# Ranking edges in layer 0 of a graph network: a row range for each partition, counted on VectorE

## The chip, the core and the metric

The kernel runs on one core of one Trainium2 chip. The metric is the device time of one launch in microseconds (us).

## The reference, cut to what matters

There are 12,500 nodes with 128 features and 412,500 edges (200,000 drawn ones in both directions, and a loop at every node), sorted by their destination `dst`. The sources `src` are in no order.

```python
x = layernorm(x + L0(x, edge_index, edge_weight))      # layer 0
x = layernorm(x + L1(x, edge_index, edge_weight, edge_attr_50))   # layer 1

# layer 0: gather by src, sum by dst
agg = segment_sum(edge_weight[:, None] * x[src], dst, N)
L0  = relu((x + agg) @ W1 + b1) @ W2 + b2

# layer 1: gather by dst, sum by src
W   = softplus_less_log2(softplus_less_log2(attr @ nn_w1.T + nn_b1) @ nn_w2.T + nn_b2) * c[:, None]
msg = W * h1[dst]                      # h1 = x @ lin1_w.T
agg = segment_sum(msg, src, N)
L1  = (h1 + agg) @ lin2_w.T + lin2_b
```

Layer 1 sums by the unsorted index `src`. So its messages are written to DRAM sorted into 98 buckets of 128 nodes (`src >> 7`), and summed from there. Which DRAM row each edge's message goes to is its rank, and the ranks are worked out while layer 0 runs.

## The kernel before

The edges are cut into 403 tiles of 1,024 edges, each tile being 8 columns (`SUB`) of 128 partitions. The edges of layer 0 are the block at L354 to L607 in `edge_network_kernel`; every engine has its own loop over the tiles, and semaphores tie them together. A tile falls nearly always into one window of 42 destination nodes. For one tile t of layer 0:

- GpSimd (POOL, L424 to L438) issues eight indirect DMAs at L434, each a gather of 128 rows of x into `xg[s]`. Gather s of tile t waits until the matmul that used `xg[s]` in tile t-1 is done (semaphore `summed`, L433), and the first gather of each half until ScalarE has written the indices `gidx` (L413).
- TensorE (PE) goes in this order: two groups of eight counting matmuls (L465 and L467, 128x100 bf16), the eight matmuls that sum the weighted rows into the window (L477; `summed` goes up by one for each), the two halves of the edge network's first layer (L483, 128x512 f32, on `attr`, which SyncE loads at L373), and three matmuls whose result nobody reads (`spin`, L631).
- ScalarE writes `gidx` (L413) and computes a softplus by Abs, Exp and Ln (L397 to L401) on the result of L483.
- VectorE (DVE, L549 to L595) makes `oha`, the one-hot of each edge's bucket (L555, 8 x 100 bf16), the one-hot of the destinations (L566, eight times), adds the window to `aggT` (L502), does the ranking (L577 to L590), writes `hid` (L509, twice), and in the first three of the four parts counts one bucket of the next part (L708).
- SyncE (SP) stores `hid` (L365), clears blocks of the table (L378) and loads `attr` (L373). They stand in program order on its queue.

The ranking before: `seen[p, b]` is the next free row of bucket b, the same in every partition. The matmuls at L465 with the strictly triangular `lower` give `above`, how many edges of bucket b lie in this tile on a lower partition. The ones at L467 with `ones16` give `in_tile`, how many there are in the tile. VectorE waits for both (semaphore `counted`, L579) and then:

```python
ahead = above + seen                    # L581, PSUM <- PSUM, SBUF
count[NB:] = pair * fixed_earlier       # L583
seen = seen + in_tile                   # L585, SBUF <- SBUF, PSUM
count[:NB] = oha * tall(ahead)          # L587, 128x800
rank = sum(count)                       # L590, 128x864 -> 128x8
```

At the start of each of the four parts of about 101 tiles, `plan_part` (PE L442 to L451, DVE L511 to L538) lays out the buckets' blocks in the table, and sets `seen` to the first row of each bucket. `counts[p, b]` holds, for each partition on its own, how many edges of bucket b its columns of that part have (L708, `count_bucket`).

Layer 1 (`layer1_edges`, L988 to the end of the function) has one tile loop too. PE computes the second layer of the edge network (L1128) and picks h1 by a one-hot (L1139); ScalarE makes a softplus (L1185 to L1189); VectorE makes the messages; POOL scatters them by rank with eight indirect DMAs a tile (L1232). From tile 105 on, the sorted rows are also summed: VectorE L1314 (one-hots, two SBUF inputs) and L1325, PE L1158.

## Time and profile before

| what | us |
|---|---|
| median of 3 runs | 11676.23 |
| lowest and highest run | 11665.03, 11705.83 |
| profiled execution, span from first to last instruction | 11664.8 |
| layer 0, edges | about 155 to 5200 |
| nodes between the layers | about 5200 to 5400 |
| layer 1, edges, without and with sums | about 5400 to 6820, 6820 to 11110 |
| layer 1, remaining sums, then nodes | about 11110 to 11665 |

The profile gives no time of the profiled execution other than its span; the span is 11.4 us below the median of the runs and equals the lowest of them within 0.3 us. Busy time is given by engine: PE is the matmul side of TensorE, PEld its weight loads, SPq are DMA issues of SyncE. In a timeline, `[3.47 <-PE bank L467]` says that the engine sat idle for 3.47 us before this instruction and what, by the profile's inference, ended that. "remote" is a releaser that the profile could not name.

### The profile page before, as it was taken

What the parts mean: (1) busy time and instruction counts of PE and PEld (TensorE: products, weight loads), DVE (VectorE), ACT (ScalarE), POOL (GpSimd) and SP (SyncE); (2) the same over time, 40 slices, a digit from 0 to 9 for tenths busy, and PEclk for the clock granted to TensorE, in tenths of its full rate; (3) what the DMA queues carried; (4) which work ended last, traced back from release to release, by engine and by line L of the source; (5) the groups of instructions that cost most, each with busy time, mean ns of one, the idle gap of its engine ahead of it and who ended that gap; (6) DMA issues with size and microseconds to landing.
All of it is one profiled execution on the core that took longest, in us unless ns stands there. A gap on an engine that the chain in (4) does not pass through costs nothing. (4 is left out here: it accounts for less than half of the span.)

```text
span 11664.8 us, 216512 instructions
## 1 busy us (share of the span) xinstructions
PE 6895.8 (59%) x38816; PEld 4956.1 (42%) x38817; DVE 6516.8 (56%) x20428; ACT 3390.7 (29%) x6781; POOL 6346.0 (54%) x6541
## 2 busy tenths in 40 slices
PE   2555566565555666665444456666666666666666
PEld 1333333333333333334232345555555555555566
DVE  7666666666666655555333345555555555555555
ACT  2333333333333333334222222222222222222202
POOL 3666566665666566652555555555555565555500
PEclk8777776777777777778776678888888888888887
DMA  3333343433333333443333344444444444444444
GB/s 101 124 121 123 119 124 122 124 121 120 122 124 121 120 124 123 124 122 123 99 100 98 100 133 150 149 149 156 150 152 146 151 156 148 157 151 151 153 155 151
DMA packets 803242, 1533.31 MB, mean 131 GB/s; under 512 B 193070, under 2 KB 206820, under 8 KB 802707
## 3 DMA queue, kind: packets, MB, share of 16 engines
q1 hardware_dynamic: 593415, 1093.58, 28.8%
q0 software_dynamic: 209456, 436.16, 13.0%
q10 hardware_dynamic: 348, 3.33, 0.1%
q14 instruction: 17, 0.14, 0.0%
q8 instruction: 6, 0.10, 0.0%
HBM read 967.92 MB, written 564.58 MB: 131 GB/s over the span
## 5 line engine op out<-in xcount | busy, mean ns | idle before, releaser
L1232 POOL DMA_INDIRECT sorted_messages<-rows,sidx x3224 | 3261.3, 1012 | 2621.7 <-DVE sidx L1279 1433.0
L434 POOL DMA_INDIRECT xg<-x_rows,gidx x3224 | 3043.0, 944 | 2134.8 <-PE bank L477 1112.7
L483 PE MATMUL bank<-attr,nn 128*128 128x512 f32 x1612 | 1494.2, 1082 | 1764.1 <-DMA attr<-attr_cols 1501.9
L1158 PE MATMUL bank<-hot,block_rows 128*128 128x128 f32 x9312 | 1586.3, 341 | 248.6 <-DVE hot L1314 140.7
L1185 ACT ACTIVATE soft<-bank 128x512 f32<-128x512 f32 x806 | 481.4, 597 | 4079.1 <-remote 2654.4
L1158 PEld LDWEIGHTS bank<-hot,block_rows 128*128 128x128 f32 x9312 | 1507.6, 254 | 299.4 <-issue 285.2
L1128 PE MATMUL bank<-w_nn2T,e_hid 128*128 128x128 f32 x6448 | 1057.4, 309 | 610.4 <-DMA e_hid<-hidden 349.0
L483 PEld LDWEIGHTS bank<-attr,nn 128*128 128x128 f32 x1612 | 468.9, 321 | 2225.7 <-issue 2061.2
L1285 DVE SCALAR_TENSOR_TENSOR rows<-filt,meta,bank 128x128 f32<-128x128 f32 x3224 | 916.6, 344 | 809.7 <-remote 534.8
L1128 PEld LDWEIGHTS bank<-w_nn2T,e_hid 128*128 128x128 f32 x6448 | 977.4, 219 | 816.7 <-DMA e_hid<-hidden 481.1
L397 ACT ACTIVATE soft<-bank 128x512 f32<-128x512 f32 x808 | 475.4, 588 | 2751.7 <-issue 1841.9
L1139 PE MATMUL bank<-h1w,ohT 128*128 128x128 bf16 x3224 | 345.3, 272 | 1429.6 <-DVE ohT L1261 959.1
L631 PE MATMUL bank<-bias_b,ones 128*128 128x512 bf16 x3627 | 1167.0, 455 | 34.8 <-issue 33.9
L477 PE MATMUL bank<-onehot,xg 128*128 128x42 f32 x6448 | 860.7, 287 | 236.1 <-DMA xg<-x_rows,gidx 199.6
L1276 DVE SCALAR_TENSOR_TENSOR filt<-bank,soft 128x512 f32<-128x512 f32 x806 | 555.6, 689 | 695.4 <-issue 349.6
L581 DVE TENSOR_TENSOR bank<-bank,seen 128x100 f32<-128x100 f32 x403 | 109.1, 271 | 1456.1 <-remote 869.2
L477 PEld LDWEIGHTS bank<-onehot,xg 128*128 128x128 f32 x6448 | 793.6, 195 | 272.5 <-DMA xg<-x_rows,gidx 227.4
L1139 PEld LDWEIGHTS bank<-h1w,ohT 128*128 128x128 bf16 x3224 | 267.6, 122 | 1498.8 <-issue 1353.5
L1314 DVE TENSOR_TENSOR hot<-cols,block_rows 128x512 f32<-128x512 f32 x1167 | 801.7, 687 | 153.1 <-DMA block_rows<-sorted_messages 111.2
L631 PEld LDWEIGHTS bank<-bias_b,ones 128*128 128x128 bf16 x3627 | 423.5, 118 | 856.3 <-issue 691.0
L566 DVE TENSOR_SCALAR onehot<-cols,rel,wgt 128x42 f32<-128x42 f32 x3224 | 729.2, 333 | 0.0
L1325 DVE TENSOR_TENSOR aggT<-aggT,bank 128x128 f32 x1164 | 330.4, 284 | 699.7 <-issue 458.6
(182 smaller groups left out, 8173.3 us busy)
## 6 DMA issues: line engine op xcount, KB each, us to landing
block_rows<-sorted_messages SPq DMA_DIRECT2D x389, 792.0 KB
hidden<-hid SPq DMA_DIRECT2D x404, 512.0 KB
e_hid<-hidden SPq DMA_DIRECT2D x403, 512.0 KB
sorted_messages<-zero SPq DMA_DIRECT2D x403, 264.0 KB
dstb<-dst SPq DMA_DIRECT2D x403, 256.0 KB
attr<-attr_cols SPq DMA_DIRECT2D x403, 204.0 KB
xg<-x_rows,gidx POOLq DMA_INDIRECT x3224
sorted_messages<-rows,sidx POOLq DMA_INDIRECT x3224
```

Of the source, the lines that this page charges most:

```text
L434: pool.indirect_dma_start(xg[s][:, :], None, x_rows, bass.IndirectOffsetOnAxis(ap=gidx[s // HALF][:, s % HALF:s % HALF + 1], axis=0),).the ...
L477: nc.tensor.matmul(bank[0][:, 0:WIN], xg[s][:, :], onehot[:, s, :], start=(s == 0), stop=(s == SUB - 1)).then_inc(summed, 1)
L483: nc.tensor.matmul(bank[2 + h][:, :], nn1[:, :], attr[:, h, :], start=True, stop=True).then_inc(z1_set, 1)
L566: ins = dve.tensor_scalar(onehot[:, s, :], cols[:, 0:WIN], rel[:, s:s + 1], wgt[:, ds(here + s, 1)], ALU.is_equal, ALU.mult)
L631: nc.tensor.matmul(unread[:, :], ones3[:, :], bias3["b2"][:, :], start=True, stop=True)
L1128: ins = nc.tensor.matmul(bank[2 + h][:, s * P:s * P + P], hid[:, h, s * P:s * P + P], nn2T[:, :], start=False, stop=(s == HALF - 1))
L1139: ins = nc.tensor.matmul(bank[4 + h][:, s * P:s * P + P], ohT[:, at:at + P], h1w[:, :], start=True, stop=True)
L1158: ins = nc.tensor.matmul(sums[u][:, 0:P], block_rows[k][:, u, s, 0:D], hot[u][:, s, :], start=(s == 0), stop=(s == HALF - 1))
L1232: pool.indirect_dma_start(table, bass.IndirectOffsetOnAxis(ap=sidx[b][h][:, s:s + 1], axis=0), rows[b][h][:, s, :], None).then_inc(landed[ ...
L1276: dve.scalar_tensor_tensor(filt[h][:, :], bank[2 + h][:, :], 0.0, soft2[h][:, :], ALU.max, ALU.add).then_inc(filt_set, 1)
L1285: ins = dve.scalar_tensor_tensor(rows[b][h][:, s, 0:D], filt[h][:, part], meta[:, ds(here + (h * HALF + s), 1), 1], bank[4 + h][:, part], ...
L1314: dve.tensor_tensor(hot[u][:, :, :], cols[:, :].rearrange("p (o n) -> p o n", o=1).broadcast_to([P, HALF, P]), block_rows[k][:, u, :, D:D ...
```

## The change

In each bucket every partition gets a row range of its own. `plan_part` gets one more matmul, f32, `lower` times `counts`: for each partition the number of edges of bucket b that lower partitions have in the whole part. `seen` starts at the bucket's first row plus that number. From then on a partition needs only its own edges: `in_tile[p, b]` is the sum of `oha` over the tile's 8 columns, a reduction on VectorE with the view turned round, and the count is `oha * seen`, with both inputs in SBUF. The sixteen matmuls at L465 and L467, the semaphore `counted` and its two waits, and the add at L581 are gone. `seen` is raised after the rank is reduced.

```diff
-PLAN_STEPS = 9
+PLAN_STEPS = 10
-        lower = sb("lower", [P, P], bf16)
+        lower = sb("lower", [P, P], f32)
...
+                in_tile, block_start = sb2("in_tile", [P, NB], f32), sb2("block_start", [P, NB], f32)
...
-                above, in_tile = bank[6][:, 0:NB], bank[6][:, P:P + NB]
-                fixed_cols, ahead = bank[7][:, 0:NB], bank[7][:, P:P + NB]
+                fixed_cols = bank[7][:, 0:NB]
...
                             pe.wait_ge(plan, PLAN_STEPS * q + 3)
+                            nc.tensor.matmul(bank[5][:, 400:400 + NB], lower[:, :], counts[:, 0:NB], start=True, stop=True)
...
-                        nc.tensor.matmul(bank[0][:, 0:WIN], lower[:, :], zero16[:, 0:WIN], start=True, stop=True).then_inc(summed, SUB)
+                        nc.tensor.matmul(bank[0][:, 0:WIN], ones16[:, :], zero16[:, 0:WIN], start=True, stop=True).then_inc(summed, SUB)
...
                                 windows = jobs.windows()
-                                pe.wait_ge(oha_set, t + 1)
-                                pe.wait_ge(seen_set, t + 1)
-                                for s in range(SUB):
-                                    nc.tensor.matmul(above, lower[:, :], oha[:, s, :], start=(s == 0), stop=(s == SUB - 1))
-                                for s in range(SUB):
-                                    ins = nc.tensor.matmul(in_tile, ones16[:, :], oha[:, s, :], start=(s == 0), stop=(s == SUB - 1))
-                                ins.then_inc(counted, 1)
                                 with pe.Fori(0, windows):
...
                             dve.wait_ge(seen_set, q * PT + 1)
-                            dve.wait_ge(ahead_set, q * PT)
-                            dve.tensor_scalar(seen[:, :], bank[5][:, 128:128 + NB], float(BLOCK), float(base_row), ALU.mult, ALU.add).then_inc(plan, 1)
+                            dve.tensor_scalar(block_start[:, :], bank[5][:, 128:128 + NB], float(BLOCK), float(base_row), ALU.mult, ALU.add).then_inc(plan, 1)
...
                             dve.wait_ge(plan, PLAN_STEPS * q + 7)
+                            dve.tensor_tensor(seen[:, :], block_start[:, :], bank[5][:, 400:400 + NB], ALU.add).then_inc(plan, 1)
...
                                 dve.wait_ge(rank_set, t + 1)
-                                dve.wait_ge(counted, t + 1)
                                 dve.tensor_tensor(oha[:, :, :], tall(fixed_cols, NB), wide(bucket16[:, ds(here, SUB)], NB),
                                                   ALU.is_equal).then_inc(oha_set, 1)
...
-                                dve.wait_ge(counted, t + 2)
                                 dve.wait_ge(seen_set, t + 1)
-                                dve.tensor_tensor(ahead, above, seen[:, :], ALU.add).then_inc(ahead_set, 1)
+                                dve.wait_ge(oha_set, t + 1)
+                                dve.tensor_tensor(count[:, :, 0:NB], oha[:, :, :], tall(seen[:, :], NB), ALU.mult).then_inc(count_set, 1)
                                 dve.wait_ge(pair_set, 2 * t + 1)
                                 dve.tensor_tensor(count[:, :, NB:PAIRS], pair[:, :, :], fixed_earlier, ALU.mult).then_inc(pair_set, 1)
-                                dve.wait_ge(ahead_set, t + 1)
-                                dve.tensor_tensor(seen[:, :], seen[:, :], in_tile, ALU.add).then_inc(seen_set, 1)
-                                dve.wait_ge(oha_set, t + 1)
-                                dve.tensor_tensor(count[:, :, 0:NB], oha[:, :, :], tall(ahead, NB), ALU.mult).then_inc(count_set, 1)
+                                dve.tensor_reduce(in_tile[:, :], oha[:, :, :].rearrange("p s n -> p n s"), axis=AX.X, op=ALU.add).then_inc(tile_set, 1)
                                 dve.wait_ge(pair_set, 2 * t + 2)
                                 dve.wait_ge(count_set, t + 1)
                                 dve.tensor_reduce(rank[:, ds(here, SUB)], count[:, :, :], axis=AX.X, op=ALU.add).then_inc(rank_set, 1)
+                                dve.wait_ge(tile_set, t + 1)
+                                dve.tensor_tensor(seen[:, :], seen[:, :], in_tile[:, :], ALU.add).then_inc(seen_set, 1)
```

## Rows read from the trace of the kernel before

**Rows 1.** The page of the profile: the span.

```profile
span 11664.8 us, 216512 instructions
```

**Rows 2.** By stretch: us, PE, PEld, DVE, ACT, POOL, each busy (x), clock, DMA, GB/s.

```profile
160.00:3912.00 3752.00, 2232.45 (x11700) 1333.32 (x11700) 2404.85 (x6614) 1200.05 (x2392) 2261.66 (x2397) 0.72 0.40 123
3912.00:5200.00 1288.00, 795.31 (x4040) 473.44 (x4039) 725.23 (x2081) 413.33 (x824) 778.18 (x824) 0.71 0.39 122
5400.00:6820.00 1420.00, 637.77 (x3329) 439.39 (x3328) 534.02 (x2179) 404.79 (x828) 798.74 (x832) 0.71 0.32 99
6820.00:11110.00 4290.00, 2720.33 (x16711) 2262.92 (x16711) 2303.32 (x8062) 1167.66 (x2388) 2461.64 (x2393) 0.81 0.48 151
```

**Rows 3.** Timeline, layer 0, two tiles: start, busy us, engine, line.

```profile
2009.85 0.52 PE L467 MATMUL bank<-oha,ones 128*128 128x100 bf16 x8
...
2011.82 0.27 DVE L581 TENSOR_TENSOR bank<-bank,seen 128x100 f32<-128x100 f32 x1 [3.47 <-PE bank L467]
...
2012.30 0.98 DVE L587 TENSOR_TENSOR count<-oha,bank 128x800 f32<-128x800 bf16 x1
2012.63 0.94 POOL L434 DMA_INDIRECT xg<-x_rows,gidx  x1 [2.73 <-PE bank L477]
...
2017.64 1.78 DVE L566 TENSOR_SCALAR onehot<-cols,rel,wgt 128x42 f32<-128x42 f32 x8
...
2020.53 0.22 DVE L577 TENSOR_TENSOR pair<-bucket 128x64 f32 x1 [0.72 <-issue]
...
2021.36 0.94 POOL L434 DMA_INDIRECT xg<-x_rows,gidx  x1 [0.30 <-issue]
...
2025.04 0.94 POOL L434 DMA_INDIRECT xg<-x_rows,gidx  x1 [2.73 <-PE bank L477]
```

**Rows 4.** Timeline, layer 0, a tile whose last gather landed late.

```profile
4426.19 0.94 POOL L434 DMA_INDIRECT xg<-x_rows,gidx  x1 [0.30 <-issue]
...
4426.79 0.52 PE L467 MATMUL bank<-oha,ones 128*128 128x100 bf16 x8
...
4429.01 0.27 DVE L581 TENSOR_TENSOR bank<-bank,seen 128x100 f32<-128x100 f32 x1 [4.03 <-remote]
...
4429.82 0.94 POOL L434 DMA_INDIRECT xg<-x_rows,gidx  x1 [2.69 <-PE bank L477]
...
4431.77 0.42 PE L477 MATMUL bank<-onehot,xg 128*128 128x42 f32 x2 [2.90 <-DMA xg<-x_rows,gidx]
```

**Rows 5.** Groups by line, layer 0, 300 to 3900 us (288 tiles).

```profile
L434 POOL DMA_INDIRECT xg<-x_rows,gidx x2303 | 2173.1, 944 | 1425.9 <-PE bank L477 789.2 <-issue 629.1 <-remote 7.3
...
L590 DVE TENSOR_REDUCE rank<-count 128x864 f32 x288 | 303.2, 1053 | 55.0 <-DVE count L587 55.0
...
L587 DVE TENSOR_TENSOR count<-oha,bank 128x800 f32<-128x800 bf16 x287 | 281.3, 980 | 0.0
...
L465 PE MATMUL bank<-oha,lower 128*128 128x100 bf16 x2304 | 178.4, 229 | 5.8 <-DVE oha L555 5.8
...
L467 PE MATMUL bank<-oha,ones 128*128 128x100 bf16 x2304 | 160.5, 215 | 0.0
...
L581 DVE TENSOR_TENSOR bank<-bank,seen 128x100 f32<-128x100 f32 x287 | 77.7, 271 | 999.7 <-remote 529.7 <-PE bank L467 469.6 <-issue 0.3
L585 DVE TENSOR_TENSOR seen<-seen,bank 128x100 f32<-128x100 f32 x287 | 73.5, 256 | 0.0
```

**Rows 6.** Group of L1314, layer 1, 6820 to 11110 us.

```profile
L1314 DVE TENSOR_TENSOR hot<-cols,block_rows 128x512 f32<-128x512 f32 x897 | 616.1, 687 | 40.9 <-issue 29.5 <-remote 11.2
```

**Rows 7.** Timeline, layer 1: a VectorE instruction with two SBUF inputs and a POOL issue.

```profile
8027.23 0.69 DVE L1314 TENSOR_TENSOR hot<-cols,block_rows 128x512 f32<-128x512 f32 x1
8027.30 1.45 POOL L1232 DMA_INDIRECT sorted_messages<-rows,sidx  x1 [0.30 <-issue]
```

**Rows 8.** Timeline, layer 0: the same meeting, with a short instruction.

```profile
4076.86 0.23 DVE L577 TENSOR_TENSOR pair<-bucket 128x64 f32 x1 [1.29 <-issue]
4076.91 0.99 POOL L434 DMA_INDIRECT xg<-x_rows,gidx  x1 [0.30 <-issue]
```

More of the change, by code:

```diff
@@ L332, in edge_network_kernel @@
                 flushed, rel_set, passed, passed_sp = sem("flushed"), sem("rel_set"), sem("passed_pool"), sem("passed_sp")
-                oha_set, counted, ahead_set, seen_set, pair_set, count_set, rank_set = (
-                    sem(n) for n in ("oha_set", "counted", "ahead_set", "seen_set", "pair_set", "count_set", "rank_set"))
-                above, in_tile = bank[6][:, 0:NB], bank[6][:, P:P + NB]
-                fixed_cols, ahead = bank[7][:, 0:NB], bank[7][:, P:P + NB]
+                oha_set, tile_set, seen_set, pair_set, count_set, rank_set = (
+                    sem(n) for n in ("oha_set", "tile_set", "seen_set", "pair_set", "count_set", "rank_set"))
+                fixed_cols = bank[7][:, 0:NB]
                 fixed_earlier = bank[7][:, 2 * P:2 * P + SUB * SUB].rearrange("p (s r) -> p s r", s=SUB)
@@ L451, in plan_part @@
                             nc.tensor.matmul(bank[4][:, 0:SLOTS], ones16[0:NB, :], at_or_past[0:NB, :], start=True, stop=True).then_inc(planned, 1)
-                        nc.tensor.matmul(bank[0][:, 0:WIN], lower[:, :], zero16[:, 0:WIN], start=True, stop=True).then_inc(summed, SUB)
+                        nc.tensor.matmul(bank[0][:, 0:WIN], ones16[:, :], zero16[:, 0:WIN], start=True, stop=True).then_inc(summed, SUB)
                         for h in range(2):
                             nc.tensor.matmul(bank[2 + h][:, :], ident[:, :], zero[:, 0:HE], start=True, stop=True).then_inc(z1_set, 1)
-                        pe.sem_inc(counted, 1)
                         jobs = TileTable(pe, "pe0", nwin)
@@ L535, in plan_part @@
                             dve.scalar_tensor_tensor(used[:, :], bank[4][:, 0:SLOTS], NB - 0.5, slot_rows[:, :], ALU.is_lt, ALU.mult).then_inc(plan, 1)
-                            dve.wait_ge(plan, PLAN_STEPS * q + 8)
+                            dve.wait_ge(plan, PLAN_STEPS * q + 9)
                             dve.tensor_single_scalar(slot_row[:, at], used[:, :], float(base_row), ALU.add).then_inc(plan, 1)
```

## The prediction

> **What bounds the kernel now.** I first cut the span of 11664.8 us [rows 1] by stretch. The change touches only layer 0, where 300 tiles (2397 gathers and their neighbours on POOL, eight a tile) take 3752 us, 12.5 us a tile, in the first three parts, and 103 tiles take 1288 us, 12.5 us again, in the last one [rows 2]. No engine is busy all the time: per tile of the first stretch PE is busy 2232.45/300 = 7.4 us, VectorE 2404.85/300 = 8.0 us, ScalarE 4.0 us, POOL 7.5 us [rows 2]. In the last part VectorE has a whole microsecond less to do (725.23/103 = 7.0 us, since L708 is gone) and the tile takes as long as before. So VectorE is not the bound, and a microsecond of slack on it is worth nothing.
>
> Then I read the timeline for what repeats. POOL's gathers stand 1.25 us apart (0.944 us busy [rows 5] and 0.30 us of issue), seven steps from 2012.63 to 2021.36 = 8.73 us, and the next tile's first gather starts 3.68 us after the last one, at 2025.04 [rows 3]. That makes 12.41 us: POOL's ring alone is the tile. POOL's idle 2.73 us is put down to PE's L477, and VectorE's 3.47 us at L581 to the counting matmuls L467. The second looks as if counting were the delay. But the counting matmuls had ended at 2009.85 + 0.52 = 2010.37, 1.45 us before L581 started [rows 3]. In another place they ended at 4427.31 and L581 started 1.70 us later [rows 4]. What stays fixed is the distance from the last gather's start: 4426.19 to L581 at 4429.01 is 2.82 us, to the next first gather 3.63 us. And that first gather (4429.82) went out before PE had even got the last gathered tile: L477 waited for it until 4431.77 [rows 4]. So the release of both comes late and together, about 2.8 us behind the last gather's start, whatever PE is doing; what holds it I can't name from the trace.
>
> **The change part by part.**
> - *Sixteen matmuls less on PE.* (178.4 + 160.5)/288 = 1.18 us a tile [rows 5]. They lie in the time in which the release is being held. Worth 0 if the release stays tied to the last gather, at most 1.18 us a tile if it is tied to PE's queue. I take 0, because rows 3 and 4 show the same 12.4 us with PE at different places.
> - *VectorE's wait for `counted` goes.* Its idle at L581 is 999.7/287 = 3.48 us a tile [rows 5]. Behind it stand the rest of the ranking, the two `hid` writes and L708, and SyncE's store of `hid` waits for those. All of it moves ahead. What is late next on VectorE is L566, which waits for the eighth `summed` of the tile before, released in the same burst. So VectorE's idle moves to L566 and PE's and SyncE's slack grows. Value: 0.
> - *VectorE's own work.* L581 goes (0.27 us). L587 keeps its 800 elements (0.98 us). L585 stays (0.26 us) with both inputs in SBUF. New is the reduction of 128x800 bf16 to 128x100 with a stride of 100 elements. No row shows it: the nearest is L590, 864 elements in 1.053 us [rows 5], which makes 0.98 us for 800; below, half of that if bf16 goes at double rate; above, twice, 2.0 us, if the stride halves the rate. I take 0.98. VectorE then has 8.03 - 0.27 + 0.98 = 8.74 us in a tile of 12.4, and at the upper bound 9.8 us. Even with some 1 us of gaps that fits, and the work is off the ring. If the cover of 3.48 us were gone, it would cost 0.71 us a tile.
> - *The layout at the start of a part.* One more f32 matmul and one more add, four times in the run. Eight bf16 matmuls of 100 columns take 0.52 us [rows 3], so one f32 one is below that, with the add (0.27 us) under 1 us: at most 4 us in all, 0 to 0.03%. I take 2 us.
> - *The operands of L587.* This is what I expect to be felt. `ahead` was in PSUM and `seen` is in SBUF, so L587 now reads two SBUF operands, and so does the add to `seen`. Before, L587 ran from 2012.30 to 2013.28 across the start of a gather at 2012.63, which took its usual 0.94 us [rows 3]. In layer 1 the instruction L1314 has both inputs in SBUF. One that ran from 8027.23 to 8027.92 had a POOL issue start within it, and that issue took 1.45 us [rows 7] where the mean without such company is 798.74/832 = 0.960 us [rows 2]: 0.49 us longer, for 0.62 us that L1314 still had to run. Layer 0 has the small version: L577, both inputs in SBUF, ran until 4077.09, and the gather that began at 4076.91 took 0.99 us and not 0.94 [rows 8]; 0.18 us left, 0.05 us paid. So an issue that starts inside such an instruction is stretched by what is left of it less about 0.13 us. Gathers are issued back to back, so each stretch lengthens the ring.
>
> How much a tile? Below: 0, if L587 fits between two starts, which stand 1.25 us apart. Above: 0.98 - 0.13 = 0.85 us. The mean comes from layer 1: with sums beside it, L1232 has 2461.64/2393 = 1.029 us against 0.960 [rows 2], so 8 x 0.069 = 0.55 us a tile, for 897/299 = 3 instructions of 0.687 us [rows 6], 2.06 us. That is 0.27 us paid for each us of such work. Here the new work is 0.98 + 0.26 = 1.24 us a tile, so 0.33 us, x 403 = 134 us. Phase: VectorE restarts at L566 when the eighth `summed` arrives, L577 comes 2.89 us after L566 (2017.64 to 2020.53 [rows 3]) and L587 a few tenths later. With the release 0.8 us before the first gather and an unknown 0.5 to 1 us from release to L566, L587 starts 2.8 to 4.0 us after the first gather. The starts in reach are at 3.74 us and 4.99 us: of that stretch about two thirds meets one. That is why I take the mean and neither end.
>
> The Trainium skill's page "SBUF — State Buffer", section "Who interferes with whom", says that a VectorE instruction with two SBUF inputs contends with a GpSimd instruction that reads SBUF, but infers that tensor_tensor does not hold up descriptor generation, which would need the write interface. The 1.45 us of a POOL issue beside L1314 speaks against that inference; by it this term would be 0 and the time that of the kernel before.
>
> Sum against the profiled execution: 11664.8 + 134 + 2 = 11801 us. The median of the runs shown is 11 us above that span, so 11812 us; I say 11810.
>
> **The rivals.**
> - *Nothing to be measured (within 0.3%, 35 us).* The ring is as before and L587 falls between two starts, or the stretch does not apply to it. For: the free place is 0.4 us of every 1.25, and the phase may lock into it. Against: rows 7 and 8. Time 11664.8 + 11 + 2 = 11678 us. By the page's inference it would be this too.
> - *Faster.* The release is tied to how far PE's queue has come, and the trace hides that. For: PE's L467 is named as releaser in half of the waits at L581 [rows 5], and L477 at POOL's. Against: 12.4 us in both places of rows 3 and 4. It decides where PE, with 1.18 us less ahead of L477, lets go earlier: up to 1.18 us a tile, 403 x 1.18 = 475 us, with the 134 us given back -341. So 11200 us to 11340 us; in part of that, anything from there to 11640 us.
> - *VectorE becomes the bound.* It would need 12.4 - 8.74 - 1 = 2.7 us more than I count, beyond the upper bound of the reduction. Or the new order puts `hid` late for PE; it comes earlier here. Slower without a clear price, 1 in 20: at twice the reduction and the worst stretch, 403 x 0.85 = 343 us, 12020 us.
> - *The change doesn't do what it says*, since the rows of a bucket are spread by partition and layer 1's scatters and sums read them in another order. The bytes and the descriptors are the same, and the table is scattered by single rows either way. I give it no price.
>
> **How the numbers follow.** 0.3% is about what a measurement of this kernel can tell from no change. Slower by the stretch: 0.41, and by VectorE 0.03, together 0.44; no difference 0.26; faster 0.30. The likeliest is the stretch at its mean, 11810 us; its own range is 11715 to 12020. The range over the cases goes from 11290, inside the faster rival, to 11960, inside the upper end of the stretch, and leaves out about 1 in 10 on either side.
>
> **What would show it.** If I am right: PE's group L465 and L467 and VectorE's L581 are gone; L566 has the long idle time instead; the mean of L434 goes from 944 ns to about 985 ns, with one gather of each tile at 1.2 to 1.7 us and L587 in progress when it starts; the last gather to the next first one stays 3.6 to 3.7 us; L1232 keeps 0.96 and 1.03 us. The stretch is wrong if the mean of L434 stays at 944 ns while the tile stays at 12.4 us. The whole picture is wrong if the distance from the last gather to the next first one drops below 3.4 us: then PE's queue held the release. The reduction is mis-sized if it takes less than 0.5 or more than 2 us.

## The result, and the profile after

The changed kernel takes 11993.99 us (11975.99 to 12027.4, four runs), the kernel before in the same comparison 11691.03 us: a ratio of 1.0255, with an interval of 1.0234 to 1.0276. It is slower by 303 us. The forecast was slower, 11810 us and at most 11960 us; the sign was right, the growth more than twice what was said (303 us for 134 us). The experiments ran on several chips, on which the kernel before had medians of 11691 to 11814 us. So only ratios to the kernel before on the same chip are compared below.

The page of the changed kernel, its span and the busy time of the engines [rows 1 has the span before, 11664.8]:

```profile
span 11975.8 us, 202418 instructions
...
PE 6920.6 (58%) x32376; PEld 4931.7 (41%) x32377; DVE 6962.6 (58%) x20432; ACT 3393.7 (28%) x6781; POOL 6430.7 (54%) x6541
```

The stretches of layer 0, columns as in [rows 2]:

```profile
160.00:3912.00 3752.00, 2135.53 (x6510) 1247.89 (x6510) 2578.88 (x6239) 1131.38 (x2252) 2184.65 (x2257) 0.64 0.36 116
3912.00:5300.00 1388.00, 807.40 (x2488) 477.64 (x2487) 897.34 (x2212) 433.67 (x862) 839.06 (x863) 0.65 0.37 119
```

In 3752 us POOL now starts 2257 instructions and not 2397, eight a tile: 282 tiles and not 300, 13.3 us a tile and not 12.5. In the last part, where VectorE has no bucket to count (L699, which was L708), it is only 12.7 us. From its first gather to its last, layer 0 takes 5310 us and not 5041: 270 us of the 311 us by which the span grew. Another 34 us lie in layer 1's scatters, from 5710 to 5743 us, and these are not clear of variation: over the runs below that stretch takes 5712 to 5802 us, whatever the edit in layer 0. A scatter costs what it did, a mean of 1.02 to 1.03 us beside the sums ([rows 2]: 1.029 us):

```profile
L1223 POOL DMA_INDIRECT sorted_messages<-rows,sidx x2371 | 2438.0, 1028 | 1835.6 <-DVE sidx L1270 986.9 <-issue 708.1 <-ACT rows L1185 132.1
```

The groups by line of layer 0, 300 to 3900 us (before: [rows 5]; L434 is the gathers, L476 the edge network, which was L483, L573 the count, which was L587, L576 the new reduction, L558 the one-hot):

```profile
L434 POOL DMA_INDIRECT xg<-x_rows,gidx x2167 | 2097.9, 968 | 1503.1 <-issue 603.0 <-ACT gidx L413 328.5 <-PE bank L470 299.1
L476 PE MATMUL bank<-attr,nn 128*128 128x512 f32 x1083 | 997.4, 1076 | 691.2 <-DMA attr<-attr_cols 486.8 <-issue 158.8 <-DVE hid L502 45.5
...
L558 DVE TENSOR_SCALAR onehot<-cols,rel,wgt 128x42 f32<-128x42 f32 x2168 | 496.0, 324 | 551.4 <-remote 466.9 <-issue 49.5 <-PE bank L470 34.9
L576 DVE TENSOR_REDUCE in_tile<-oha 128x100 f32<-128x800 bf16 x271 | 407.1, 1502 | 0.0
...
L573 DVE TENSOR_TENSOR count<-oha,seen 128x800 f32<-128x800 bf16 x271 | 267.1, 986 | 1.7 <-issue 1.7
```

To be read here: the gathers have a mean of 968 ns and not 944 (0.19 us a tile), and 2167 of them fit in 3600 us, against 2303. Their idle time is no longer all at one place. Before, PE's L477 ended 789 us of it and no ScalarE line stood there; now L413 (`gidx`) ends 328 us. The reduction takes 1.50 us, a half more than the 0.98 us I took.

The stretch is there, as foretold, though not in every tile: a gather starts within L573 in 185 of the 403 tiles. L573 (two SBUF inputs) and such a gather:

```profile
2005.39 0.98 DVE L573 TENSOR_TENSOR count<-oha,seen 128x800 f32<-128x800 bf16 x1
...
2005.57 1.63 POOL L434 DMA_INDIRECT xg<-x_rows,gidx  x1 [0.31 <-issue]
```

What is new is in this timeline. The first gathers of three tiles are those at 2098.61, 2119.24 and 2129.87, so one tile took 20.6 us and the next 10.6 us:

```profile
2098.47 0.71 SPq L378 DMA_DIRECT2D sorted_messages<-zero  x1
...
2098.61 0.94 POOL L434 DMA_INDIRECT xg<-x_rows,gidx  x1 [0.30 <-issue]
...
2102.36 0.94 POOL L434 DMA_INDIRECT xg<-x_rows,gidx  x1 [0.30 <-issue]
2105.54 0.29 SPq L373 DMA_DIRECT2D attr<-attr_cols  x1
2105.59 0.23 DVE L545 TENSOR_SCALAR rel<-dstf,basef 128x8 f32 x1 [2.84 <-issue]
...
2106.33 0.94 POOL L434 DMA_INDIRECT xg<-x_rows,gidx  x1 [3.03 <-remote]
...
2111.86 3.78 PE L476 MATMUL bank<-attr,nn 128*128 128x512 f32 x4 [11.24 <-issue]
...
2113.96 0.60 ACT L397 ACTIVATE soft<-bank 128x512 f32<-128x512 f32 x1 [13.64 <-PE bank L476]
...
2118.15 0.46 ACT L413 ACTIVATE gidx<-srci 128x4 int32 x2 [0.46 <-issue]
...
2119.24 0.94 POOL L434 DMA_INDIRECT xg<-x_rows,gidx  x1 [8.22 <-ACT gidx L413]
...
2128.62 0.94 POOL L434 DMA_INDIRECT xg<-x_rows,gidx  x1 [0.30 <-issue]
...
2129.87 0.94 POOL L434 DMA_INDIRECT xg<-x_rows,gidx  x1 [0.30 <-issue]
```

SyncE's `attr` load (L373) goes out 7.07 us after its block clear (L378). PE gets to L476 only at 2111.86, after 11.24 us of idle time, ScalarE's softplus waits for that 13.64 us, `gidx` stands behind the softplus in ScalarE's order, and the next tile's first gather goes out at 2119.24 after 8.22 us. Before, this gap was 2.7 us in the tiles shown [rows 3, 4]. This long tile is no exception. I call the standard deviation of the tile lengths between 300 and 3900 us their spread: it was 0.6 us before and is 3.0 us now. Nine tiles in ten lay between 12.4 and 12.7 us and now lie between 10.0 and 19.1 us. Nor is it only the gap ahead of the first gather. On average the distance from a tile's last gather to the next first one even falls, from 3.7 to 3.4 us, while the seven steps between a tile's own gathers grow from 8.8 to 9.9 us, of which the stretch is 0.2 us. A gap of over 1 us stands between a tile's own gathers in 40% of the tiles, before in 4%. So the even tile of 12.4 us has given way to short and long tiles with a mean of 13.3 us.

### The profile page after: what moved, and what is told of

Same layout as the page of the kernel before. It is cut to its first block and busy times, and to the rows that moved or that the text cites. A ratio compares the mean times of both kernels' runs of the same rounds, so it can differ in the third digit from the quotient of the medians.

```text
span 11975.8 us, 202418 instructions
## 1 busy us (share of the span) xinstructions
PE 6920.6 (58%) x32376; PEld 4931.7 (41%) x32377; DVE 6962.6 (58%) x20432; ACT 3393.7 (28%) x6781; POOL 6430.7 (54%) x6541
## 5 line engine op out<-in xcount | busy, mean ns | idle before, releaser
L434 POOL DMA_INDIRECT xg<-x_rows,gidx x3224 | 3127.5, 970 | 2321.7 <-issue 1038.1
L476 PE MATMUL bank<-attr,nn 128*128 128x512 f32 x1612 | 1478.5, 1072 | 958.3 <-DMA attr<-attr_cols 695.7
L470 PE MATMUL bank<-onehot,xg 128*128 128x42 f32 x6448 | 1250.7, 348 | 1307.1 <-DMA xg<-x_rows,gidx 584.5
L470 PEld LDWEIGHTS bank<-onehot,xg 128*128 128x128 f32 x6448 | 1161.4, 257 | 1564.3 <-issue 882.8
L558 DVE TENSOR_SCALAR onehot<-cols,rel,wgt 128x42 f32<-128x42 f32 x3224 | 736.1, 324 | 886.3 <-remote 746.4
L476 PEld LDWEIGHTS bank<-attr,nn 128*128 128x128 f32 x1612 | 469.6, 321 | 1402.6 <-issue 1203.4
L576 DVE TENSOR_REDUCE in_tile<-oha 128x100 f32<-128x800 bf16 x403 | 605.5, 1503 | 0.0
```

The source lines that it names most:

```text
L434: pool.indirect_dma_start(xg[s][:, :], None, x_rows, bass.IndirectOffsetOnAxis(ap=gidx[s // HALF][:, s % HALF:s % HALF + 1], axis=0),).the ...
L470: nc.tensor.matmul(bank[0][:, 0:WIN], xg[s][:, :], onehot[:, s, :], start=(s == 0), stop=(s == SUB - 1)).then_inc(summed, 1)
L476: nc.tensor.matmul(bank[2 + h][:, :], nn1[:, :], attr[:, h, :], start=True, stop=True).then_inc(z1_set, 1)
L558: ins = dve.tensor_scalar(onehot[:, s, :], cols[:, 0:WIN], rel[:, s:s + 1], wgt[:, ds(here + s, 1)], ALU.is_equal, ALU.mult)
L576: dve.tensor_reduce(in_tile[:, :], oha[:, :, :].rearrange("p s n -> p n s"), axis=AX.X, op=ALU.add).then_inc(tile_set, 1)
```

## The experiments

Three theories stood at the start: the stretched gathers are the whole loss (1); the rhythm that VectorE's wait gave is lost (2); the longer reduction is what costs (3). Later ones came from the first results: PE's work ahead of L470 or its lateness (4), the matmuls themselves (5), the waits tied to them (6).

In the table, "tile" is 3600 us x 8 / the number of gathers that start between 300 and 3900 us, and "spread" the standard deviation of the distance between the first gathers of successive tiles there. The granted clock is TensorE's in the same stretch. "PE ahead of L470" leaves out the three matmuls of the spin, which every run but a_free16_nospin has there too. A free matmul waits for nothing, and nothing waits for it.

| run | PE ahead of L470 | VectorE | ratio (interval) | tile, us | spread, us | clock |
|---|---|---|---|---|---|---|
| before | 16 counting | waits twice | 1 | 12.5 | 0.6 | 0.72 |
| after | none | no wait | 1.0255 (1.0234 to 1.0276) | 13.3 | 3.0 | 0.64 |
| a_seen_psum | none | `seen` in PSUM | 1.0207 (1.017 to 1.0244) | 13.2 | 3.2 | 0.64 |
| a_wait_back | 1, with waits | waits twice | 1.0318 (1.0282 to 1.0354) | 13.7 | 3.7 | 0.65 |
| a_both | 1, with waits | waits twice, PSUM | 1.0394 (1.0354 to 1.0434) | 13.7 | 3.8 | 0.65 |
| a_matmuls_back | 16, with waits | waits once | 0.997 (0.9951 to 0.9989) | 12.5 | 0.5 | 0.71 |
| a_mb_psum | 16, with waits | waits once, PSUM | 0.9986 (0.9974 to 0.9999) | 12.5 | 0.5 | 0.70 |
| a_mb_wait | 16, with waits | waits twice | 1.0026 (1.0011 to 1.004) | 12.7 | 0.6 | 0.71 |
| a_more_spin | 3 more of 512 columns | no wait | 1.0094 (1.0076 to 1.0113) | 12.9 | 2.4 | 0.69 |
| a_pe_late | an idle wait | no wait | 1.0178 (1.0161 to 1.0195) | 13.1 | 2.5 | 0.62 |
| b_ahead_sbuf | 16 counting | waits twice, two SBUF inputs | 1.0092 (1.0071 to 1.0112) | 12.8 | 0.6 | 0.70 |
| a_mb_free | 16 on zeros, free | no wait | 0.9993 (0.9977 to 1.0009) | 12.6 | 0.6 | 0.70 |
| a_one_matmul | 1, with waits | waits once | 1.0215 (1.0188 to 1.0241) | 13.3 | 3.0 | 0.65 |
| a_one_spin | 1 with waits, 3 of 512 | waits once | 1.0063 (1.0038 to 1.0087) | 12.9 | 2.2 | 0.70 |
| a_tiny16 | 16 of 4 columns | no wait | 0.9992 (0.9973 to 1.001) | 12.6 | 0.7 | 0.64 |
| a_free8 | 8 on zeros | no wait | 0.9975 (0.9961 to 0.9988) | 12.5 | 1.1 | 0.68 |
| a_free16_nospin | 16 in place of the spin | no wait | 0.9981 (0.9967 to 0.9994) | 12.6 | 0.7 | 0.65 |
| a_free32 | 32 on zeros | no wait | 1.0043 (1.0026 to 1.006) | 12.8 | 0.4 | 0.76 |
| a_tiny16_behind | 16 of 4 columns, behind L470 | no wait | 1.0544 (1.0521 to 1.0566) | 14.3 | 3.0 | 0.62 |
| a_tiny8_psum | 8 of 4 columns | no wait, PSUM | 0.994 (0.992 to 0.9961) | 12.5 | 0.9 | 0.65 |

### First: the stretch, the wait, the matmuls

a_seen_psum:

```diff
-                fixed_cols = bank[7][:, 0:NB]
+                fixed_cols, seen = bank[7][:, 0:NB], bank[7][:, P:P + NB]
```

> The changed kernel with seen kept in PSUM, so that L573 and the add to seen read one SBUF operand each. Theory 1 (the stretch of the gathers and what follows from it is the whole loss): the gathers' mean goes from 970 ns back to 944 ns and the time to 11690 to 11730 us. Theory 2 (the loss is mostly the lost rhythm: VectorE no longer waits for PE, works at another time in the tile, and the gathers wait irregularly for PE and ScalarE): only the 85 us of longer gathers come back, 11890 to 11920 us, and the irregular gaps in front of the gathers stay. Theory 3 (VectorE's 1.5 us reduction is the rest): 11890 to 11920 us too.

```profile
L434 POOL DMA_INDIRECT xg<-x_rows,gidx x2183 | 2066.3, 947 | 1534.1 <-issue 621.1 <-PE bank L470 324.1 <-remote 322.9
L476 PE MATMUL bank<-attr,nn 128*128 128x512 f32 x1091 | 1001.7, 1073 | 675.3 <-DMA attr<-attr_cols 507.4 <-issue 148.0 <-DVE hid L502 19.7
```

The gathers are at 947 ns and the time falls only from 1.0255 to 1.0207. The stretch alone is not the loss. The gathers' idle time is as scattered as before the edit, and the spread is 3.2 us.

a_wait_back, on the changed kernel:

```diff
                                 windows = jobs.windows()
+                                pe.wait_ge(oha_set, t + 1)
+                                pe.wait_ge(seen_set, t + 1)
+                                nc.tensor.matmul(bank[6][:, P:P + NB], ones16[:, :], oha[:, 0, :], start=True, stop=True).then_inc(counted, 1)
...
                                 dve.wait_ge(rank_set, t + 1)
+                                dve.wait_ge(counted, t + 1)
...
+                                dve.wait_ge(counted, t + 2)
                                 dve.wait_ge(seen_set, t + 1)
```

> The changed kernel with the old waits back: PE does one 128x100 matmul where the sixteen stood and posts counted, VectorE waits for it ahead of L573. Theory 2: the rigid ring is back (gap ahead of the first gather 2.7 us in every tile, the other gaps 0.30 us), but L573 then runs across the start of the first gather in every tile and stretches it by up to 0.85 us: 11690 + 300 to 340 = 11990 to 12030 us, with a tile of 13.2 us and nothing irregular. Theory 1: the same stretch, so the same time; the two differ by the run with both edits. Theory 3: VectorE now also has its wait: above 12100 us.

The ratio is 1.0318. An even ring under theory 2 was to show a tile of 13.2 us with nothing irregular; the tile is 13.7 us and its spread 3.7 us, so the ring is not back.

a_both has the edits of a_wait_back and a_seen_psum.

> Both edits: the wait back and seen in PSUM. Theory 2: the ring and the gathers are as before the change, 11690 us within 0.3%. Theory 1: 11690 to 11730 us, the same as seen in PSUM alone. Theory 3 (the reduction is what costs): about 11900 us, since its 1.5 us is still there.

```profile
L435 POOL DMA_INDIRECT xg<-x_rows,gidx x2095 | 1978.0, 944 | 1624.3 <-issue 630.4 <-PE bank L475 365.4 <-ACT gidx L414 331.1
L481 PE MATMUL bank<-attr,nn 128*128 128x512 f32 x1048 | 956.8, 1065 | 1296.3 <-DMA attr<-attr_cols 922.1 <-issue 272.7 <-DVE hid L507 101.0
```

With all waits back and gathers of 944 ns it is 1.0394, slower than the change itself and than any of the three theories had foretold for this run. Theory 2, that VectorE's wait gave the rhythm, falls, and theory 1 a second time: the tile is 13.7 us without any stretch.

a_matmuls_back has the sixteen in place of the one, on `ones16` and `oha`, into a bank that nobody reads, and not the last of the three edits (no wait ahead of the ranking).

> The changed kernel with the sixteen counting matmuls back on PE, their results unread, and no wait of VectorE ahead of the ranking (only ahead of the next one-hot). If PE's work itself set the rhythm or the clock, the time goes back towards 11690 us. Theories 1 to 3: it stays at 11990 us, or goes up to 12050 us since PE has 1.2 us more in each tile.

```profile
L435 POOL DMA_INDIRECT xg<-x_rows,gidx x2311 | 2279.1, 986 | 1323.9 <-PE bank L479 677.9 <-issue 559.8 <-ACT gidx L414 61.2
L485 PE MATMUL bank<-attr,nn 128*128 128x512 f32 x1156 | 1061.9, 1074 | 41.9 <-DMA attr<-attr_cols 38.4 <-DVE hid L511 3.4
...
L586 DVE TENSOR_REDUCE in_tile<-oha 128x100 f32<-128x800 bf16 x289 | 441.6, 1528 | 0.0
```

The whole loss is gone, 0.997, though the gathers are longer than ever (986 ns) and the reduction takes 1.53 us. The spread is 0.5 us again. Theories 1 to 3 all fall here. What the change lost is something that the counting matmuls gave as matmuls.

PE's wait for `attr` ahead of the edge network is not the mark of the loss, though it falls from 487 us (L476) to 38 us (L485) here. In the kernel before, which is even, it was the longest of the three:

```profile
L483 PE MATMUL bank<-attr,nn 128*128 128x512 f32 x1152 | 1070.9, 1085 | 1360.4 <-DMA attr<-attr_cols 1203.2 <-issue 143.4 <-DVE hid L509 13.8
```

### Second: work, lateness, and what the stretch costs

a_more_spin:

```diff
-SPIN0 = 3
+SPIN0 = 6
```

> The changed kernel with six matmuls of 128x512 bf16 whose result nobody reads behind each tile's edge network on PE, where it has three. Theory 4 (what the change lost is the PE work that stood between the edge network and L470: with it the granted clock stays up, or PE comes to L470 later, at the moment that suits the semaphores): the three add about the time of the sixteen counting matmuls, and the time goes back to 11680 us within 0.5%, the granted clock from 0.64 to 0.72 in layer 0. If the counting matmuls mattered in another way (their wait for the one-hot), it stays at 11990 us or above.

a_pe_late:

```diff
                                     pe.wait_ge(onehot_ready, j + 1)
+                                    pe.wait_ge(tile_set, t + 1)
```

> The changed kernel where PE waits, idle, for VectorE's reduction L576 of the same tile before L470, so it comes to L470 later without more work. If the lateness of PE is what the counting matmuls gave: back to about 11700 us, with the granted clock still at 0.64. If it was the work and the clock: 11990 us or above.

The gathers of a_pe_late and its stretch of 300 to 3900 us, columns as in [rows 2]:

```profile
L434 POOL DMA_INDIRECT xg<-x_rows,gidx x2201 | 2156.9, 980 | 1443.2 <-issue 568.4 <-PE bank L471 561.4 <-remote 286.9
```

```profile
300.00:3900.00 3600.00, 2138.03 (x6249) 1283.01 (x6349) 2500.93 (x6076) 1104.99 (x2203) 2156.89 (x2201) 0.62 0.38 117
```

A PE that is only late wins back a third (1.0178), one with three more long matmuls two thirds (1.0094); both lie between what the theories foretold. Neither this lateness nor that amount of work is enough. In a_pe_late the wait also ties PE to VectorE in a new way, so it doesn't show lateness by itself.

a_mb_psum (a_matmuls_back and a_seen_psum together):

> The changed kernel with the sixteen matmuls back and seen in PSUM. That kernel with seen in SBUF took 11678 us though its gathers were stretched to a mean of 982 ns, 123 us in all. If POOL's issues are in the ring, 11560 us; if POOL has slack there and another loop sets 12.4 us, 11680 us within 0.3%, with a gap ahead of the first gather that is longer by the 0.3 us a tile that the stretch took.

Gathers of 946 ns, the same tile of 12.5 us: in this order the stretch of 0.3 us a tile was hidden in the gap ahead of the first gather, whose mean is 2.73 us here and 2.43 us in a_matmuls_back.

b_ahead_sbuf, on the kernel before:

```diff
-                fixed_cols, ahead = bank[7][:, 0:NB], bank[7][:, P:P + NB]
+                fixed_cols = bank[7][:, 0:NB]
+                ahead_sb = sb2("ahead_sb", [P, NB], f32)
+                ahead = ahead_sb[:, :]
```

> The kernel before with ahead in SBUF and not in PSUM, so that L587 reads two SBUF operands at its old place, across the start of each tile's first gather, and nothing else changes. Theory 1 in its strict form (a stretched gather lengthens POOL's ring by what it is stretched): the first gather goes from 0.94 to about 1.5 us and the time to 11720 + 403 x 0.5 to 0.6 = 11920 to 11960 us. If another loop sets the pace: 11720 us within 0.3%, though the first gather is longer.

The timeline of one tile, and the group of the gathers:

```profile
2009.40 0.98 DVE L589 TENSOR_TENSOR count<-oha,ahead_sb 128x800 f32<-128x800 bf16 x1
2009.74 1.46 POOL L436 DMA_INDIRECT xg<-x_rows,gidx  x1 [2.56 <-PE bank L479]
```

```profile
L436 POOL DMA_INDIRECT xg<-x_rows,gidx x2246 | 2263.7, 1008 | 1336.6 <-PE bank L479 718.0 <-issue 604.5 <-remote 12.6
```

This is the stretch by itself: the same instruction at the same place, with both inputs in SBUF, takes the first gather from 0.94 us [rows 3] to a mean of 1.46 us, over 1.4 us in 99% of the tiles. 0.52 us x 403 = 210 us of longer gathers cost 0.92%, some 108 us: half of it is hidden, since the tile grows by 0.3 us only (12.5 to 12.8), part of it by a shorter gap ahead of that gather (2.56 us, not 2.73). On the page's inference that I weighed (Trainium skill, "SBUF — State Buffer", "Who interferes with whom": tensor_tensor does not hold up descriptor generation), the trace disagrees.

### Third: the matmuls or their waits

a_mb_free:

```diff
                                 windows = jobs.windows()
+                                for s in range(2 * SUB):
+                                    nc.tensor.matmul(bank[6][:, 0:NB], ones16[:, :], zero16[:, 0:NB], start=True, stop=True)
```

> The changed kernel with sixteen 128x100 bf16 matmuls on PE where the counting ones stood, on constant zeros, without any wait and with no one waiting for them. Theory 5 (it is the matmuls themselves, their work between the spin and L470): as with the sixteen real ones, a ratio to before of 0.997 to 1.003. Theory 6 (it is the waits of PE for the one-hot and for seen, or VectorE's wait for counted ahead of the one-hot, that keep the engines in step): it stays at a ratio of 1.02 or above, or at the 1.009 of the longer spin.

```profile
L434 POOL DMA_INDIRECT xg<-x_rows,gidx x2285 | 2210.2, 967 | 1391.4 <-PE bank L472 738.6 <-issue 595.0 <-ACT gidx L413 30.0
```

a_one_matmul is a_matmuls_back with one in place of sixteen.

> As the kernel with the sixteen matmuls back (PE waits for the one-hot and seen, VectorE waits for counted ahead of the next one-hot, none ahead of the ranking), but one matmul in place of sixteen. Theory 5: a ratio of 1.02 to 1.03. Theory 6: 0.997 to 1.003.

```profile
L435 POOL DMA_INDIRECT xg<-x_rows,gidx x2158 | 2095.8, 971 | 1508.3 <-issue 636.4 <-PE bank L475 329.9 <-remote 285.7
```

Sixteen matmuls on zeros, with no wait on either side: 0.9993. One matmul with the waits: 1.0215. What the change lost is the matmuls, not their waits.

a_one_spin is a_one_matmul with `SPIN0 = 6`:

> As the one above, with six unread 128x512 matmuls a tile in place of three: the waits and about the columns of the sixteen. If waits and work each give a part: a ratio of 0.997 to 1.003. Theory 5 with only the number of columns counting: 1.009, as the longer spin alone.

Its interval (1.0038 to 1.0087) overlaps that of the longer spin alone (1.0076 to 1.0113): these waits give little or nothing.

a_mb_wait is a_matmuls_back with the wait `dve.wait_ge(counted, t + 2)` ahead of L573 too:

> The sixteen matmuls back and VectorE's wait for counted ahead of the ranking back too, so that only the reduction, the two SBUF operands and the order are new. With the wait, L573 runs across the start of each tile's first gather, as in the kernel before with ahead in SBUF: a ratio of 1.009 from that, and if the 1.5 us reduction costs where VectorE waits for PE, more: the tile then holds the chain L573 to the hid writes behind the release, 1.2 us longer than before, for a ratio up to 1.04. If VectorE has slack there: 1.009.

```profile
L435 POOL DMA_INDIRECT xg<-x_rows,gidx x2267 | 2154.3, 950 | 1446.6 <-PE bank L479 824.3 <-issue 619.2 <-ACT gidx L414 3.1
```

1.0026, and not the 1.009 or more that I expected. The stretch that was to give 1.009 is missing: the gathers have a mean of 950 ns, so the count (L573, here L584) is nearly over when the first gather starts. And the 1.5 us reduction behind the old wait costs nearly nothing. PE waits 1154 us for `attr` in this run, in even tiles, as before the change.

### Fourth: what about the matmuls

a_tiny16 is a_mb_free with 4 columns for `NB` in both operands, a_free8 and a_free32 have 8 and 32 for `2 * SUB`, and a_free16_nospin leaves the line `spin(nc, bank[1], ones3, bias3, SPIN0)` out.

> Sixteen free matmuls on the changed kernel as in a_mb_free, but of 4 columns each in place of 100: the same sixteen weight loads and instructions, 1/25 of the columns. If the number of matmul instructions and weight loads ahead of L470 is what counts: a ratio of 0.997 to 1.003. If it is the columns, the time or the clock they hold up: 1.015 to 1.03.

Gathers, the tiny matmuls, and the stretch of 300 to 3900 us, columns as in [rows 2]:

```profile
L434 POOL DMA_INDIRECT xg<-x_rows,gidx x2279 | 2204.7, 967 | 1397.5 <-PE bank L472 757.0 <-issue 594.5 <-ACT gidx L413 27.0
...
L463 PE MATMUL bank<-zero,ones 128*128 128x4 bf16 x4544 | 160.1, 166 | 0.0
```

```profile
300.00:3900.00 3600.00, 2269.12 (x10820) 1441.01 (x11105) 2589.76 (x6286) 1141.06 (x2275) 2204.25 (x2279) 0.64 0.38 121
```

64 columns in all, the granted clock at 0.64 as in the changed kernel, and the time is back (0.9992). So it isn't the columns and not the clock. By the profile the sixteen keep PE busy for 160.1/285 = 0.56 us a tile.

> Eight free matmuls of 100 columns in place of sixteen. If the effect goes by dose: halfway, a ratio of 1.01 to 1.015. If there is a threshold that eight reach: 1.000; if not: 1.02 or above.

Eight do as much as sixteen in the time, though the spread is 1.1 us with eight and 0.6 us with sixteen (a_mb_free). If the spin's three are counted too, PE has 3, 4, 6, 7 and 11 matmuls between L476 and the next tile's L470 in the changed kernel, a_one_matmul, a_more_spin, a_one_spin and a_free8, and the ratios are 1.0255, 1.0215, 1.0094, 1.0063 and 0.9975. So the effect goes with the number of matmul instructions and the time gains no more beyond eight added ones. Their columns don't sort the runs: 3072 in a_more_spin, 2336 in a_free8.

> Sixteen free matmuls of 100 columns (1600 columns) in place of the three of 512 columns (1536), on the changed kernel. If the kind of work counts (many short matmuls with weight loads): 1.00 to 1.01. If the total of PE's work in that place counts: as the change, 1.02 to 1.03.

The same columns as the three long matmuls of the changed kernel, in sixteen instructions: 0.9981 against 1.0255.

> Thirty-two free matmuls of 100 columns on the changed kernel. If more of it helps more: a ratio under 0.99, and the granted clock of layer 0 above 0.72. If the gain ends where the regular ring of 12.4 us is reached: 1.000; if PE becomes late by it: above 1.005.

1.0043, between two of the three cases. The clock rises to 0.76 and the kernel is slower than with sixteen: more is only more work. A higher clock buys nothing here.

### Last: the place, and the best version

a_tiny16_behind:

```diff
                                     jobs.step()
+                                for s in range(2 * SUB):
+                                    nc.tensor.matmul(bank[6][:, 0:4], ones16[:, :], zero16[:, 0:4], start=True, stop=True)
                                 for h in range(2):
                                     pe.wait_ge(attr_in, 16 * (t + 1))
```

> The sixteen 4-column matmuls of a_tiny16 moved to the place between L470 and the edge network L476. If the number of PE instructions in the tile loop is what counts, wherever they stand: 0.997 to 1.003. If they must stand behind the spin and ahead of L470, whose wait for the last gather they keep PE from: 1.015 to 1.03.

```profile
L434 POOL DMA_INDIRECT xg<-x_rows,gidx x2013 | 1980.7, 984 | 1619.8 <-ACT gidx L413 740.2 <-issue 566.2 <-remote 160.4
```

The same sixteen instructions behind L470 and ahead of the edge network: 1.0544, a tile of 14.3 us, far outside both cases. The number in the loop is not what counts, and nor is the loop's length in instructions, which is that of a_tiny16. They help ahead of L470 and harm between L470 and L476.

a_tiny8_psum has eight 4-column matmuls ahead of L470, and `seen` in PSUM:

> The version that the runs point to: the changed kernel, eight 4-column matmuls ahead of L470 and seen in PSUM. Ring as before and gathers of 944 ns: a ratio of 0.995 to 1.001. It beats the kernel before only if POOL's shorter gathers are in the ring of this version; in a_mb_psum they were not.

Its groups:

```profile
L434 POOL DMA_INDIRECT xg<-x_rows,gidx x2305 | 2180.8, 946 | 1419.9 <-PE bank L472 713.4 <-issue 624.7 <-remote 41.4
...
L578 DVE TENSOR_REDUCE in_tile<-oha 128x100 f32<-128x800 bf16 x288 | 437.5, 1519 | 0.0
```

0.994 (0.992 to 0.9961): 0.6% faster than the kernel before, a little more than I expected. The gathers are at 946 ns, and PE's L472 ends half of their idle time again. By the condition that I had set, POOL's shorter gathers are in the ring of this version; a_free8, which has the stretch, is at 0.9975. SyncE's order tells nothing: from a block clear to the next `attr` load it takes 4.1 us on average here, 4.7 us in the changed kernel, and 2.9 us before.

## Why the prediction had the sign right and the cause wrong

- **The sixteen matmuls, taken at 0.** This step failed. I reasoned that they lay in time in which the release was held anyway, since the tile was 12.4 us with PE at two different places [rows 3, 4]. That showed that PE's lateness by a microsecond did not matter in the kernel as it stood. It did not show that the pace would hold without them: both places had the matmuls in. Their loss costs 2.2% with the stretch gone (a_seen_psum against a_mb_psum, 1.0207 and 0.9986), and 2.6% with it (1.0255 against 0.9993, a_mb_free). That is nearly the whole of the change, on a term that I had priced at 0 to 1.18 us a tile of gain.
- **POOL's ring as the tile.** Also wrong as I put it. The gap of 2.7 us ahead of the first gather was to stay; in the timeline above it is 8.22 us in one tile and 0.30 us, back to back, in the one behind it. The test I named, a distance from a tile's last gather to the next first one below 3.4 us, is met in 62% of the tiles and was met in 3% before. Its mean falls, so on average the whole loss lies between a tile's own gathers. A second path to the next first gather, by `attr`, PE's L476, ScalarE's softplus and `gidx`, I had not drawn. The long tile above goes along it, and `gidx` ends 328 us of POOL's idle time. How much of the loss goes along it is not shown.
- **The stretch.** Right in kind, and the rule holds: in 148 tiles a gather starts with 0.2 us or more of L573 still to run, and each takes longer by that remainder less 0.13 us. The add to `seen` (L581) hardly counts; a gather that starts within it takes 0.99 us on average. In size it was less than I took: (970 - 944) ns x 3224 = 84 us of longer gathers over all of layer 0, where I had 134 us. I gave two thirds for L573 meeting a start (my own figures, 0.94 of 1.2 us, make it nearer four fifths), and it is 185 of 403 tiles. I had reckoned with a fixed order within the tile, which the uneven tiles don't have. In the time it is worth about 0.5% in the changed kernel (1.0255 against 1.0207, whose intervals just overlap), nothing with the sixteen back (0.997 with it, 0.9986 without), and 0.92% where it strikes the first gather (b_ahead_sbuf). So the forecast had the right sign by luck: the term that gave it carries at most about a fifth of the loss.
- **The reduction.** 1.50 us, inside my bounds of 0.49 and 2.0 us, and off the path once the sixteen are back: at 1.53 us in a_matmuls_back the time is 0.997. What it costs in the uneven tiles of the changed kernel no run tells.
- **VectorE's wait.** Taken at 0. Against a_matmuls_back, restoring it costs 0.0056; so taking it away was worth about half a per cent, once the matmuls were back. With one matmul in their place it is worth 1% (a_wait_back against a_one_matmul, 1.0318 and 1.0215).
- **The rivals.** The faster one asked whether PE's queue held the release. It does matter, but with the other sign. VectorE as the bound is excluded by the idle time at L558, 551 us in 271 tiles, and by a_matmuls_back. Its work may still cost something in the uneven tiles. Without L699's 1.05 us, in the last part, the changed kernel's tile is 12.7 us and not 13.3, and in a_wait_back 12.9 and not 13.7. But a_more_spin has 12.9 in both, and the kernel before and a_matmuls_back have 12.5 in both. No run took L699 away by itself. The rival by which layer 1 reads the new order of rows more slowly finds no support: its scatters take 5743 us, and 5785 us in b_ahead_sbuf, which has the old order.
- **What would show it.** L558's idle time is 2.0 us a tile, where L581's was 3.5 us. The mean of the gathers is 970 ns, near the 985 ns I named, but in more than half of the tiles L573 meets no start. The test for "the whole picture is wrong" is met, as said; the cause I gave beside it (PE's queue let go earlier) would make the tiles short, and explains only those that are.

**What stays open** is how the instructions act. Shown: at least eight matmul instructions ahead of L470, of 4 or 100 columns, without any wait, make the tiles even and take the loss away. Excluded by runs: the columns, the clock, the waits as what was lost; a PE that waits idle for VectorE wins back a third. Not tried: eight instructions on PE that are not matmuls, and the same eight a few instructions earlier or later.

The traces hold one sign more. They also record the sequencers' own instructions (register arithmetic, branches, semaphore waits), which the rows above leave out. The median of one is 0.03 to 0.05 us. But between 300 and 3900 us some of them take 0.6 to 0.8 us each, mostly 0.70 us:

| run | SyncE | VectorE | POOL | ScalarE | PE |
|---|---|---|---|---|---|
| before | 861 | 54 | 0 | 0 | 0 |
| after | 839 | 527 | 140 | 92 | 0 |
| a_tiny16 | 346 | 323 | 2 | 0 | 0 |

The hole in the timeline above, 2101.3 to 2105.5 us, is made of them: VectorE has four there, SyncE three, POOL and ScalarE two each. In the nine runs with a spread above 2 us, POOL and ScalarE have 77 to 294 of them together, in the other eleven 32 at most. So the uneven tiles go together with these slow instructions on POOL and ScalarE. Which brings about the other, and what the eight matmuls do to it, no run here shows.

## What to carry to other kernels

A constant period shows what the loop does as it stands, not which of its parts is free to go. Look at the spread of the period too, and not only at its mean. Before costing a removed part at zero, replace it by something of the same shape that does nothing: sixteen dead matmuls would have told in one run. A short instruction can be worth more where it stands than for its work, and its place decides the sign. And where VectorE multiplies two SBUF operands beside POOL's DMA issues, keep one in PSUM: it paid 0.9% here where the first gather of the tile was struck, and nothing in a_mb_psum.

## What the runs showed of the hardware that was not expected

- Sixteen PE matmuls of 64 columns in all change this kernel by 2.6% one way and, moved behind L470, by 2.9% the other way (1.0255 to 0.9992 and to 1.0544).
- Register, branch and semaphore instructions with a median of 0.03 to 0.05 us at times take 0.70 us each, on several engines at once (the table above).
- A higher granted clock brought no gain: 0.9992 at 0.64 (a_tiny16), 1.0043 at 0.76 (a_free32).
- A reduction of 128x800 bf16 along a stride of 100 elements takes 1.50 us, where L590 reads 864 f32 elements in a row in 1.05 us [rows 5].
- A POOL DMA issue that starts inside a two-SBUF VectorE instruction took 1.46 us in b_ahead_sbuf, where it takes 0.94 us beside the same instruction with one input in PSUM [rows 3]. In the changed kernel such an issue takes longer by what is left of L573 less 0.13 us, and one already running when L573 starts does not (a mean of 0.95 us, 234 of them).
